# Reordering the way from the last MLP half to the mixture-of-slots layer in a two-layer transformer kernel

## The chip, the cores and the metric

One core of one Trainium2 chip runs the whole program in one launch, all data in float32 (a few tiles are rounded for TensorE). The metric is device time in microseconds (us), the median of several executions.

## The reference

Four sequences (batches) of 1024 tokens with 256 channels pass two layers; each layer's two blocks have the form x = x + gate * f(h), where h is the layer norm of x, scaled and shifted by six rows that a condition vector gives.

- Layer 0: causal softmax attention with 16 heads of 64, then a low-rank MLP with gelu.
- Layer 1, first block: layer norm, linear-time attention (relu features, prefix sums), a residual, layer norm, and an MLP y = gelu(y @ w1 + b1) @ w2 + b2 with 1024 hidden channels.
- Layer 1, second block (the "experts"): tokens are taken in groups of 16. For each group and each of 64 slots the token with the largest logit is chosen, processed and given back:

```
logits = einsum('...btd,des->...btes', grouped, controller) + tie
perm   = (logits == max(logits over the 16 tokens))
sel    = einsum('...btd,...btes->...besd', grouped, perm)
inner  = relu(einsum('...besd,...desf->...besf', sel, f1) + bias)
inter  = einsum('...besf,esfd->...besd', inner, f2)
out    = einsum('...besd,...btes->...btd', inter, perm)
```

The change lies between the MLP and the product with f1.

## The kernel before, in words

The program is written out for four batches, one after the other. `batch(b, carry)` builds one. Every instruction is recorded by `do` of one of five lanes (`pe`, `act`, `dve`, `pool`, `sp`, one an engine), in the order in which the builder calls them, and that is the order on the engine. A step's extra arguments are the steps it waits for; a lane counts its needed steps in one semaphore. There is no planner: the order in which the lines stand sets everything.

A batch has 8 tiles of 128 tokens; a half has 4. For the experts the tiles are grouped as LOW (0 to 3), MIDDLE (4, 5) and HIGH (6, 7). PSUM has 8 banks. `Banks.take` hands them out in turn and gives the step that last read the bank; whoever writes into it waits for that reader. In the traces a bank is named "bank" or "scores", the normalised rows `xn` lie in "hx", as does `h`, `hT3` is "hT", the weights w1 and w2 are "w", the hidden tile is "hid", f1 and f2 are "f", and the logits lie in "inter".

The stretch in question, per batch, in the order of the lines:

- `mlp_wide(1, ...)` (products recorded at L446, gelu at L1011): 8 blocks of hidden channels for tiles 4 to 7. One matmul of the program appears as two records, so a block is 4 records of 512 columns.
- L1512: ScalarE runs an Exp of one column into `spare_column`. Nobody reads it; in front of it the compiler puts the load of the table for Exp, which the next batch's softmax needs. Gelu uses another table; Identity, Copy and Relu need no load in either.
- L1513 `choices(LOW, slot_turn(LOW, ...))`: `turn` transposes the four normalised tiles on TensorE (L420, 4 tiles x 2 channel halves c = 0, 1, one bank for each c), ScalarE copies each bank out with scale and bias (L427). Then `choices` multiplies by the controller (L446, 4 records of 512 columns), and VectorE adds the tie row (L1398), takes the maximum (L1402) and compares (L1403), which gives `permT`. `choice_blocks` (L1413) makes masked copies for the end of the block.
- `mlp_tile(t)` (L1575): 8 matmuls, 16 records of 256 columns, over the hidden channels m = 0 to 7; it is a generator that yields after half of them and at the end. `residual` (L980, L981) then multiplies by the gate row and adds to x on VectorE.
- `spread_choices` (L1526, L1530): turns permT back, one transpose a tile, and VectorE writes `perm`.
- `chosen_rows(tiles, c, ...)` (L1549): 32-row matmuls of `h` by `perm` into four banks, which ScalarE (L1563) or VectorE (L1565) copy into `sel`. For LOW it is called for c = 0 and c = 1 apart, with four ScalarE copies of 128x512 each; for MIDDLE and HIGH with both c at once, eight copies of 128x256, four an engine.
- Norm statistics (L283 to L286 on VectorE), the power -0.5 on GpSimd (L287), the normalisation (L294), `slot_rows_of` (L1381 on VectorE, L1383 on GpSimd), for MIDDLE after tiles 4 and 5, for HIGH after 6 and 7.
- The first expert product (L1629) waits for every copy into `sel`; the second is at L1657. SP loads the next batch's x behind the HIGH logits (`turned_read`).

The order before: wide products, table load, LOW turn and logits, tile 4, LOW spread, tile 5, norm of MIDDLE, tile 6, MIDDLE turn, half of tile 7, MIDDLE logits, rest of tile 7, statistics of HIGH, MIDDLE spread, LOW rows c = 0, LOW rows c = 1, HIGH turn, HIGH logits, MIDDLE rows, HIGH spread, HIGH rows, first expert product.

Of the kernel before, what the change touches and what calls it, by code (L numbers as in the profile page):

```python
# [10 lines left out]
ACT = mybir.ActivationFunctionType  # L11
ALU = mybir.AluOpType
# [6 lines left out]
C = D // P  # L19
# [3 lines left out]
TH = T // NH  # L23
# [23 lines left out]
GT = P // NE  # L47
# [60 lines left out]
def build(nc, I, out):  # L108
# [34 lines left out]
    minus_half = sb("minus_half", [P, T])  # L143
# [3 lines left out]
    h, xn = hx[:, 0:T, :], hx[:, T:2 * T, :]  # L147
# [257 lines left out]
    def batch(b, carry):  # L405
# [4 lines left out]
        banks = Banks(all_banks)  # L410
        banks.readers, banks.at = list(carry["readers"]), carry["at"]

        def turn(src, half, ready, dst, scale=None, bias=None, after=None, tiles=None):


            copies, tiles = [], list(tiles or tiles_of(half))
            for c in range(C):
                i, ps, reader = banks.take()
                for n, (t, r) in enumerate(zip(tiles, ready)):
                    done = pe.do(lambda e, n=n, t=t, c=c, ps=ps: nc.tensor.transpose(  # L420
                        ps[:, n * P:(n + 1) * P], src[:, t, c * P:(c + 1) * P], ident[:, :]), r, reader)
                ps = ps[:, 0:len(tiles) * P]
                o = dst[:, c, tiles[0] * P:(tiles[-1] + 1) * P]
                if scale is None:
                    copy = act.do(lambda e, o=o, ps=ps: nc.scalar.copy(o, ps), done, after)
                else:
                    copy = act.do(lambda e, o=o, ps=ps, c=c: nc.scalar.activation(  # L427
                        o, ps, ACT.Identity, bias=bias[:, c:c + 1], scale=scale[:, c:c + 1]), done, after)
                banks.read_by(i, copy)
                copies.append(copy)  # L430
            return copies
# [941 lines left out]
                last = e.dma_start(f2[k * EF:(k + 1) * EF, :, :], f2_dram[k]).then_inc(loaded["f2"], 16)  # L1373
            return last

        def slot_turn(tiles, normed):
            return turn(xn, None, normed, hT3, scale=mod_cols[:, 1, 4, :, b], bias=mod_cols[:, 1, 3, :, b], tiles=tiles)

        def slot_rows_of(tiles, normed):

# [27 lines left out]
        def choice_blocks(tiles):  # L1408

            cols = columns(tiles)  # L1410
            for k in range(2):
                view = [a[:, cols].rearrange("p (q two t) -> p q two t", two=2, t=NE)[:, :, k, :] for a in (blockT, permT)]
                step = dve.do(lambda e, view=view, k=k: nc.vector.tensor_scalar(  # L1413
                    view[0], view[1], half_mask[:, k:k + 1], None, op0=ALU.mult), perm_done[tiles[0]])
            block_done.update({t: step for t in tiles})
# [93 lines left out]
        slots_normed = [normalise(x, 0, mlp_output(0, wide0), EPS)]  # L1509
        slots_h = slot_rows_of(LOW, slots_normed[0])  # L1510
        wide1 = mlp_wide(1, mlp_turn(1, mlp_norms[1]))
        act.do(lambda e: nc.scalar.activation(spare_column[:, :], minus_half[:, 0:1], ACT.Exp))  # L1512
        choices(LOW, slot_turn(LOW, slots_normed[0]))  # L1513
        choice_blocks(LOW)


        sel_done, sel_product = [], []

        def spread_choices(tiles):

# [17 lines left out]
        def chosen_rows(tiles, c, ready, engines):  # L1538

            half, first = tiles[0] // TH, tiles[0] % TH  # L1540
            taken = [banks.take() for r in range(QR)]

            def emit(e):
                for n, t in enumerate(tiles):
                    for k, cc in enumerate(c):
                        for r, (i, ps, reader) in enumerate(taken):
                            rows_ = slice(r * VPAD, (r + 1) * VPAD)
                            at_ = (k * len(tiles) + n) * P
                            last = nc.tensor.matmul(ps[:, at_:at_ + P], h[rows_, t, cc * P:(cc + 1) * P],  # L1549
                                                    perm[half][rows_, first + n, :, :].rearrange("p g s -> p (g s)"),  # L1550
                                                    start=True, stop=True)
                return last

            done = pe.do(emit, *ready, *[reader for i, ps, reader in taken])
            sel_product.append(done)
            yield
            for r, (i, ps, reader) in enumerate(taken):
                at_ = half * TH * GT + r * 2 * TH + 2 * first
                for k, cc in enumerate(c):
                    o = sel[:, cc, :, at_:at_ + 2 * len(tiles)]  # L1560
                    src = ps[:, k * len(tiles) * P:(k + 1) * len(tiles) * P].rearrange("p (k s) -> p s k", s=ES)
                    if engines[r] == "act":
                        copy = act.do(lambda e, o=o, src=src: nc.scalar.copy(o, src), done)  # L1563
                    else:
                        copy = dve.do(lambda e, o=o, src=src: nc.vector.tensor_copy(o, src), done)  # L1565
                banks.read_by(i, copy)
                sel_done.append(copy)

        def mlp_tile(t):

# [9 lines left out]
            banks.read_by(i, read)  # L1580
            yield wrote

        *_, wrote4 = mlp_tile(TH)
        low_spread = spread_choices(LOW)
        *_, wrote5 = mlp_tile(TH + 1)
        middle_normed = norm_apply(x, norm_stats(x, 1, [wrote4, wrote5], EPS, tiles=MIDDLE))
# [5 lines left out]
        choices(MIDDLE, middle_turned)  # L1592
        wrote7 = next(last_tile)
        inv = norm_stats(x, 1, [wrote6, wrote7], EPS, tiles=HIGH)
        middle_spread = spread_choices(MIDDLE)
        choice_blocks(MIDDLE)
        high_normed = norm_apply(x, inv)
        [*chosen_rows(LOW, (0,), [low_spread, *slots_h], ("act", "act", "act", "act"))]
        second_low = chosen_rows(LOW, (1,), [], ("act", "act", "act", "act"))
        next(second_low)  # L1600
        high_turned = slot_turn(HIGH, high_normed)
        high_h = slot_rows_of(HIGH, high_normed)
        [*second_low]
        turned_read = choices(HIGH, high_turned)
# [16 lines left out]
        for blk in range(4):  # L1621
            i, ps, reader = banks.take()

            def first_product(e, blk=blk, ps=ps):
                for q in range(8):
                    for c in range(C):
                        for k in range(2):
                            s = k * EP + blk * 8 + q
                            last = nc.tensor.matmul(ps[k * EF:(k + 1) * EF, q * G:(q + 1) * G], f1[:, c, s, :], sel[:, c, s, :],  # L1629
                                                    start=c == 0, stop=c == C - 1)  # L1630
                return last

            done = pe.do(first_product, reader, *(sel_done + [(loaded["f1"], 32 * (b + 1))] if blk == 0 else []))
            dst = before_relu[:, blk * 8:blk * 8 + 8, :]
            biased = dve.do(lambda e, ps=ps, dst=dst, blk=blk: nc.vector.tensor_tensor(
                dst, ps.rearrange("p (q g) -> p q g", q=8),
                fbias[:, blk * 8:blk * 8 + 8].unsqueeze(2).to_broadcast([P, 8, G]), op=ALU.add), done)
            banks.read_by(i, biased)

            relu = act.do(lambda e, dst=dst, blk=blk: nc.scalar.activation(  # L1640
                inner[:, blk * 8:blk * 8 + 8, :], dst, ACT.Relu), biased)
            inner_done.append(relu)
# [135 lines left out]
```

## Time and profile before

| | us |
|---|---|
| median of 3 runs | 1891.25 (1889.34 to 1897.14) |
| profiled execution | 1892.87, its span 1891.6 |
| TensorE (PE) busy in the span | 1770.2 |
| VectorE (DVE) busy | 1259.8 |
| ScalarE (ACT) busy | 897.1 |
| GpSimd (POOL) busy | 698.3 |
| mean granted TensorE clock | 0.988 of full speed |

The terms of a sum come from the profiled execution, so they are taken off its own time. In a row of the timeline the columns are: start and duration in us, engine, line, operation, output<-inputs, shapes and count; brackets give the idle time before it and what ended it. Rows of successive instructions of one kind are merged into one.

### The profile page before, as it was taken

How to read it: one execution, taken by the hardware profiler on the slowest of the kernel's cores; microseconds unless marked ns; L12 is line 12 of the kernel's file. 1: busy time of each engine (PE TensorE's matmuls, PEld its weight loads, DVE VectorE, ACT ScalarE, POOL GpSimd, SP SyncE). 2: the span in 40 equal slices, each digit the busy share in tenths (PEclk: the TensorE clock that was granted, in tenths of full speed). 3: DMA queues.
4: the chain of work that ended last, by engine and by line, in shares of the span. 5: the costliest groups of instructions: out<-in, count | busy, mean ns of one | idle time of the engine just before them, and what ended most of it. 6: DMA issues, size and time to landing. Idle time of an engine off the chain costs nothing.

```text
span 1891.6 us, 41279 instructions
## 1 busy us (share of the span) xinstructions
PE 1770.2 (94%) x16417; PEld 1256.2 (66%) x16417; DVE 1259.8 (67%) x2767; ACT 897.1 (47%) x1971; POOL 698.3 (37%) x1090
## 2 busy tenths in 40 slices
PE   7999998998989999999899999999989999999998
PEld 4766785666666667565856666756685666765667
DVE  4688857634688885762578888476367888757545
ACT  4476724223466672423256766242245676533223
POOL 2355543040055564213115555323112555521410
PEclk9899999999999999999999999999999999999999
DMA  8566650050256664023136666303114666520500
GB/s 227 121 153 158 142 159 16 2 89 26 80 143 145 146 139 152 1 37 54 35 95 147 146 142 141 126 1 69 21 36 124 147 147 145 135 98 1 90 1 24
DMA packets 128561, 182.65 MB, mean 97 GB/s; under 512 B 33297, under 2 KB 89329, under 8 KB 127345
## 3 DMA queue, kind: packets, MB, share of 16 engines
q1 hardware_dynamic: 114928, 173.72, 38.0%
q10 hardware_dynamic: 13440, 6.30, 1.2%
q8 instruction: 130, 2.13, 0.5%
q14 instruction: 63, 0.51, 0.1%
HBM read 62.44 MB, written 4.24 MB: 35 GB/s over the span
## 4 chain that ended last, share of the span: by engine, by line
PE 61%; SPq 15%; DVE 12%; ACT 5%; DMA 4%; issue 2%; POOL 0%; DVEq 0%; POOLq 0%
SPq L940 15%; PE scores L446 12%; PE bank L446 7%; PE bank L654 6%; PE scores L634 5%; PE bank L691 4%; DVE prob L768 4%; DMA placed<-prob 3%; PE scores L1657 2%; PE scores L1575 2%; PE scores L1045 2%; ACT prob L868 2%; PE scores L1102 2%; PE scores L1221 1%; PE bank L707 1%
## 5 line engine op out<-in xcount | busy, mean ns | idle before, releaser
L868 ACT ACTIVATE prob<-prob,neg_max 128x768 f32<-128x768 f32 (+5 forms) x384 | 273.6, 714 | 95.3 <-DVE neg_max L760 95.3
L654 PEld LDWEIGHTS bank<-placed,v_t 128*64 128x64 f32 x4608 | 252.3, 137 | 92.9 <-issue 92.9
L654 PE MATMUL bank<-placed,v_t 128*64 128x128 f32 x4608 | 274.4, 275 | 32.6 <-DMA placed<-prob 24.6
L634 PE MATMUL scores<-k_t,q_t 64*128 64x128 f32 (+10 forms) x2176 | 287.9, 410 | 0.0
L287 POOL TENSOR_TENSOR rstd<-rstd,minus_half 128x2 f32<-128x2 f32 x96 | 69.5, 725 | 574.8 <-DVE rstd L286 574.4
L768 DVE STREAM_TRANSPOSE prob<-prob 128x1536 f32<-128x1536 f32 x128 | 225.3, 1772 | 29.6 <-ACT prob L868 28.8
L830 POOL COPY placed<-prob 32x768 f32<-32x768 f32 x256 | 210.8, 823 | 19.6
L634 PEld LDWEIGHTS scores<-k_t,q_t 64*128 64x128 f32 x2176 | 165.0, 187 | 71.8 <-issue 61.2
L760 DVE CUSTOM_DVE_ANT_1 prob<-scores,hx 128x128 f32<-128x128 f32 (+4 forms) x320 | 165.3, 576 | 54.3 <-PE scores L634 34.0
L817 POOL COPY rec_wide<-rec 128x128 f32<-128x128 f32 x256 | 65.4, 291 | 329.5 <-DVE rec L772 232.8
L868 ACT ACTIVATE hx<-hx,neg_max 128x896 f32<-128x896 f32 (+1 forms) x128 | 119.5, 934 | 77.4 <-DVE neg_max L760 76.7
L760 DVE CUSTOM_DVE_ANT_1 hx<-scores,hx 128x896 f32<-128x896 f32 (+1 forms) x128 | 114.8, 953 | 51.8 <-PE scores L634 46.3
L768 DVE STREAM_TRANSPOSE hx<-hx 128x1536 f32<-128x1536 f32 x64 | 110.5, 1760 | 9.9 <-ACT hx L868 9.8
L830 POOL COPY placed<-hx 32x768 f32<-32x768 f32 x128 | 105.4, 823 | 9.7
L691 PE MATMUL bank<-hT,w_ring 128*128 128x512 f32 x224 | 103.6, 605 | 0.0
L1011 ACT ACTIVATE hid<-scores,b 128x512 f32<-128x512 f32 x96 | 62.9, 694 | 64.2 <-PE scores L446 64.2
L980 DVE TENSOR_TENSOR tmp<-bank,mod_rows 128x256 f32<-128x256 f32 x26 | 11.0, 425 | 122.1 <-PE bank L1031 64.0
L446 PE MATMUL scores<-mT,w 128*128 128x512 f32 x192 | 85.8, 596 | 3.5 <-ACT mT L427 3.5
L839 POOL TENSOR_TENSOR yT<-yT,tmp 128x256 f32<-128x256 f32 (+1 forms) x64 | 46.1, 730 | 113.5 <-ACT yT L881 113.5
L881 ACT COPY yT<-bank 128x256 f32<-128x256 f32 (+2 forms) x128 | 44.0, 369 | 84.5 <-PE bank L654 84.4
L760 DVE CUSTOM_DVE_ANT_0 prob<-scores,hx 128x1024 f32<-128x1024 f32 x64 | 75.8, 1222 | 6.6 <-PE scores L634 6.6
L1230 DVE TENSOR_TENSOR am<-scores,tril 128x512 f32<-128x512 f32 x112 | 69.9, 683 | 11.8 <-PE scores L1221 8.7
(246 smaller groups left out, 3330.3 us busy)
## 6 DMA issues: line engine op xcount, KB each, us to landing
placed<-prob SPq DMA_DIRECT2D x768, 96.0 KB, 2.2
placed<-hx SPq DMA_DIRECT2D x384, 96.0 KB, 2.1
f<-in_L_ffn_f SPq DMA_DIRECT2D x16, 2048.0 KB, 13.3
x<-in_L_attn_x SPq DMA_DIRECT2D x8, 512.0 KB, 4.3
mod_rows<-mod_scratch SPq DMA_DIRECT2D x32, 128.0 KB, 5.7
out<-x SPq DMA_DIRECT2D x16, 256.0 KB, 2.2
w_ring<-in_L_attn_w_q ACTq DMA_DIRECT2D x24, 128.0 KB, 2.9
w_ring<-in_L_attn_w_kv_up ACTq DMA_DIRECT2D x48, 64.0 KB, 2.2
```

The source lines that it names most:

```text
L287: step = pool.do(lambda e, ts=ts: nc.gpsimd.tensor_tensor(rstd[:, ts], rstd[:, ts], minus_half[:, ts], op=ALU.pow), var, filled)
L446: step = pe.do(lambda e, n=n, w=w, m=m: nc.tensor.matmul(ps, w, m, start=n == 0, stop=n == len(pieces) - 1), copy, *after)
L634: last = nc.tensor.matmul(score_tiles[head][:, at_ // 512, at_ % 512:at_ % 512 + count], q_t[buf][rows_, tile * P:(tile + 1) * P], k_of[bu ...
L654: last = nc.tensor.matmul(out_bank[rows_, at_:at_ + P], v_t[pair % 2][:, j, rows_], placed[m % 2][:, :, head, first_block(m, i) + j, :], s ...
L691: last = nc.tensor.matmul(ps, ring[:, c * P:(c + 1) * P], hT[:, c, cols], start=c == 0, stop=c == C - 1)
L760: nc.vector.tensor_tensor_reduce(prob[m % 3][:, :, head, blocks, :].rearrange("p g n i -> p g (n i)"), src.rearrange("p (g m) -> p g m", g ...
L768: nc.vector.transpose(p_, p_).then_inc(flow["shuffled"], 1)
L817: last = nc.gpsimd.tensor_copy(rec_wide[:, out_slot(m, tile), :].rearrange("p (a n) -> p a n", a=HEADS), rec[:, at_:at_ + HEADS].unsqueeze ...
L830: nc.gpsimd.tensor_copy(placed[m % 2][rows_, g, :, :, :], prob[m % 3][rows_, g, :, :, :]).then_inc(flow["kept"], 1)
L868: nc.scalar.activation(p_, p_, ACT.Exp, scale=-1.0, bias=neg_max[:, k:k + 1], accum_out=row_sum[:, k:k + 1]).then_inc(flow["exp_done"], 1)
L940: e.dma_start(placed[m % 2][target * GROUP:(target + 1) * GROUP, source, :, :, :], prob[m % 3][source * GROUP:(source + 1) * GROUP, target ...
L1230: masked.append(dve.do(lambda e, r=r, ps=ps: nc.vector.tensor_tensor(am[t % 2][:, r * 4:r * 4 + 4, :], ps.rearrange("p (h n) -> p h n", h= ...
```

## The change

- `turn` and `slot_turn` have a new argument `shared`; with it the bank of c = 1 is copied by VectorE (tensor_scalar with a scale and a bias column) and not by ScalarE. Only the HIGH turn sets it.
- The LOW turn stays where it was. Behind it now stands the first half of tile 4, then LOW logits and blocks, then the table load, then the rest of tile 4.
- The LOW rows for c = 0 stand ahead of the MIDDLE spread.
- `sel_done` is kept by c, and the copies into `sel` run over c outside and banks inside; a bank's reader is its last copy. The first expert product waits for all of them, as before.

```diff
-        def turn(src, half, ready, dst, scale=None, bias=None, after=None, tiles=None):
+        def turn(src, half, ready, dst, scale=None, bias=None, after=None, tiles=None, shared=False):
...
                 if scale is None:
                     copy = act.do(lambda e, o=o, ps=ps: nc.scalar.copy(o, ps), done, after)
+                elif shared and c:
+                    copy = dve.do(lambda e, o=o, ps=ps, c=c: nc.vector.tensor_scalar(
+                        o, ps, scale[:, c:c + 1], bias[:, c:c + 1], op0=ALU.mult, op1=ALU.add), done, after)
                 else:
...
-        act.do(lambda e: nc.scalar.activation(spare_column[:, :], minus_half[:, 0:1], ACT.Exp))
-        choices(LOW, slot_turn(LOW, slots_normed[0]))
-        choice_blocks(LOW)
-        sel_done, sel_product = [], []
+        low_turned = slot_turn(LOW, slots_normed[0])
+        sel_done, sel_product = {c: [] for c in range(C)}, []
...
-            for r, (i, ps, reader) in enumerate(taken):
-                at_ = half * TH * GT + r * 2 * TH + 2 * first
-                for k, cc in enumerate(c):
+            for k, cc in enumerate(c):
+                for r, (i, ps, reader) in enumerate(taken):
+                    at_ = half * TH * GT + r * 2 * TH + 2 * first
...
-                banks.read_by(i, copy)
-                sel_done.append(copy)
+                    banks.read_by(i, copy)
+                    sel_done[cc].append(copy)
...
-        *_, wrote4 = mlp_tile(TH)
+        first_tile = mlp_tile(TH)
+        next(first_tile)
+        choices(LOW, low_turned)
+        choice_blocks(LOW)
+        act.do(lambda e: nc.scalar.activation(spare_column[:, :], minus_half[:, 0:1], ACT.Exp))
+        wrote4 = next(first_tile)
         low_spread = spread_choices(LOW)
...
         inv = norm_stats(x, 1, [wrote6, wrote7], EPS, tiles=HIGH)
+        [*chosen_rows(LOW, (0,), [low_spread, *slots_h], ("act", "act", "act", "act"))]
         middle_spread = spread_choices(MIDDLE)
         choice_blocks(MIDDLE)
         high_normed = norm_apply(x, inv)
-        [*chosen_rows(LOW, (0,), [low_spread, *slots_h], ("act", "act", "act", "act"))]
         second_low = chosen_rows(LOW, (1,), [], ("act", "act", "act", "act"))
         next(second_low)
-        high_turned = slot_turn(HIGH, high_normed)
+        high_turned = slot_turn(HIGH, high_normed, shared=True)
...
-            done = pe.do(first_product, reader, *(sel_done + [(loaded["f1"], 32 * (b + 1))] if blk == 0 else []))
+            done = pe.do(first_product, reader, *(sel_done[0] + sel_done[1] + [(loaded["f1"], 32 * (b + 1))] if blk == 0 else []))
```

## Rows read from the trace of the kernel before

**Rows 1.** The page, busy us (share of the span) and instructions of each engine.
```profile
PE 1770.2 (94%) x16417; PEld 1256.2 (66%) x16417; DVE 1259.8 (67%) x2767; ACT 897.1 (47%) x1971; POOL 698.3 (37%) x1090
```

**Rows 2.** Timeline of ScalarE, batch 0, behind the last gelu.
```profile
428.36 1.28 ACT L1512 ACT_TABLE_LOAD   x1
429.65 0.20 ACT L1512 ACTIVATE spare_column<-minus_half 128x1 f32<-128x1 f32 x1
429.76 1.43 ACT L427 ACTIVATE hT<-scores,mod_cols 128x512 f32<-128x512 f32 x2
445.93 1.02 ACT L427 ACTIVATE hT<-scores,mod_cols 128x256 f32<-128x256 f32 x2 [14.74 <-PE scores L420]
```

**Rows 3.** Timeline of TensorE, from the low transposes to the low spread, batches 0 and 2.
```profile
427.45 1.04 PE L420 MATMUL scores<-ident,hx 128*128 128x128 f32 x8
...
437.64 0.46 PE L1526 MATMUL scores<-ident,permT 64*128 64x64 f32 x4
...
1356.28 1.04 PE L420 MATMUL scores<-ident,hx 128*128 128x128 f32 x8
1359.41 1.98 PE L446 MATMUL bank<-hT,ctrl 128*128 128x512 f32 x4 [2.09 <-ACT hT L427]
1361.23 3.62 PE L1575 MATMUL bank<-w,hid 128*128 128x256 f32 x16
1364.78 0.46 PE L1526 MATMUL scores<-ident,permT 64*128 64x64 f32 x4
```

**Rows 4.** Busy us by stretch: total, PE, PEld, DVE, ACT, POOL, then granted clock, DMA.
```profile
431.00:434.00 3.00, 3.00 (x5) 1.11 (x4) 0.00 (x0) 0.19 (x1) 0.00 (x0) 0.50 0.00 0
1359.40:1364.80 5.40, 5.39 (x21) 3.74 (x21) 2.69 (x5) 0.62 (x1) 0.00 (x0) 1.00 0.00 0
1387.00:1390.00 3.00, 1.47 (x28) 1.17 (x24) 2.16 (x8) 1.20 (x4) 0.00 (x0) 0.50 0.53 179
1390.00:1393.00 3.00, 2.82 (x53) 2.85 (x55) 0.32 (x2) 0.00 (x0) 0.00 (x0) 0.50 0.02 5
```

**Rows 5.** Timeline, VectorE behind the low logits (batch 2), and middle permT and spread (batch 0).
```profile
1361.43 0.69 DVE L1398 TENSOR_TENSOR inter<-bank,tie 128x512 f32<-128x512 f32 x1 [13.84 <-PE bank L446]
...
1362.88 0.69 DVE L1403 TENSOR_TENSOR permT<-inter,logit_max 128x512 f32<-128x512 f32 x1
...
449.66 0.42 DVE L1403 TENSOR_TENSOR permT<-inter,logit_max 128x256 f32<-128x256 f32 x1
450.36 0.33 PE L1526 MATMUL bank<-ident,permT 64*128 64x64 f32 x2
```

**Rows 6.** Timeline of TensorE, batch 0, from second low rows to first expert product.
```profile
453.11 0.38 PE L1549 MATMUL scores<-perm,hx 32*128 32x128 f32 x2 [1.31 <-DVE perm L1530]
...
454.22 0.66 PE L420 MATMUL scores<-ident,hx 128*128 128x128 f32 x4
455.31 1.16 PE L446 MATMUL scores<-hT,ctrl 128*128 128x256 f32 x4 [0.44 <-ACT hT L427]
457.31 0.39 PE L1549 MATMUL scores<-perm,hx 32*128 32x128 f32 x3 [0.84 <-ACT sel L1563]
...
458.41 0.33 PE L1526 MATMUL bank<-ident,permT 64*128 64x64 f32 x2
459.33 1.17 PE L1549 MATMUL scores<-perm,hx 32*128 32x128 f32 x32 [0.58 <-DVE perm L1530]
462.23 5.20 PE L1629 MATMUL scores<-sel,f 128*64 128x64 f32 x128 [1.73 <-DVE sel L1565]
```

**Rows 7.** The same stretch: timeline of ScalarE and VectorE, and L1565's durations.
```profile
454.69 1.02 ACT L427 ACTIVATE hT<-scores,mod_cols 128x256 f32<-128x256 f32 x2 [0.78 <-PE scores L420]
...
458.54 1.20 ACT L1563 COPY sel<-scores 128x256 f32<-128x256 f32 x4 [0.89 <-PE bank L1549]
...
453.46 0.74 DVE L294 TENSOR_SCALAR hx<-x,mv,rstd 128x256 f32<-128x256 f32 x2
...
L1565 DVE COPY sel<-scores x24: 414/415/425, 459.1 to 1850.4; 128x256 f32<-128x256 f32 x24
```

More of the change, by code:

```diff
@@ L1374, in load_f2, with slot_turn @@
             return last
-        def slot_turn(tiles, normed):
-            return turn(xn, None, normed, hT3, scale=mod_cols[:, 1, 4, :, b], bias=mod_cols[:, 1, 3, :, b], tiles=tiles)
+        def slot_turn(tiles, normed, shared=False):
+            return turn(xn, None, normed, hT3, scale=mod_cols[:, 1, 4, :, b], bias=mod_cols[:, 1, 3, :, b], tiles=tiles,
+                        shared=shared)
         def slot_rows_of(tiles, normed):
```

## The prediction

> **What bounds the kernel now.** I read the page first: busy time by engine and the chain that ended last. TensorE is busy 94% of the span [rows 1] and heads the chain too, so time can only be won where it stands still or runs at the low clock. The change touches one place, which the program passes four times (once a batch): from the last wide products of the second MLP half to the first expert product. So I then read the timeline of that place, engine by engine, in batch 0 (about 427 to 462 us) and in batch 2, and last the granted clock.
>
> Three things are to be seen. First, ScalarE: behind the last gelu stand a table load of 1.28 us and its column of 0.20, and only then the two copies of the turned rows [rows 2]. TensorE idles 2.09 us for the first of them, in all four batches alike [rows 3]. Second, TensorE's clock: in batch 0, behind that idle time, 431 to 434 us ran at 0.50 of full speed, the lower of the two levels (1.2 of 2.4 GHz); batch 1 shows the same. In batch 2 the same idle time was followed by full clock [rows 3, 4], as in batch 3. From the start of the eight transposes to that of the spread transposes took 10.19 us in batches 0 and 1 and 8.50 in 2 and 3 [rows 3]: one fall of the clock costs 1.69 us. Third, the tail from 453 to 462 us is a chain of short handovers PE, ACT, PE, DVE, with TensorE idle 1.31, 0.44, 0.84, 0.58 and 1.73 us [rows 6, 7]. It too is followed by a low clock, in each of the four batches (batch 2's rows are shown) [rows 4].
>
> **Part 1: table load behind the logits, half an MLP tile ahead of them.** I work in batch 2, which has no fall here. The transposes end at 1357.32. Products start about 0.16 before their forerunner's modelled end (logits end 1361.39, the tile starts 1361.23), so the first half of tile 4 starts at 1357.16. It is 8 of 16 products; the tile takes 3.55 us up to the next group [rows 3], so the half takes 1.78: to 1358.94. Its gelu inputs, m 0 to 3, are long done. Meanwhile ScalarE starts the copies right behind the last gelu. In batch 0 that is 428.36, and both take 1.43, to 429.79, where the logits would be reached at 428.49 - 0.16 + 1.78 = 430.11 [rows 2, 3]. The half tile therefore hides both copies with 0.3 us over, and the 2.09 us of idle time goes. The logits take 1.98: end 1360.92. VectorE follows 0.04 later, and add, maximum and comparison take 2.14 (1361.43 to 1362.88 + 0.69) [rows 5]: permT at 1363.10. The second half tile ends at about 1360.76 + 1.78 = 1362.54, so now **permT is late**, where before the full tile covered it. From permT's end to the spread transposes it was 0.28 in the middle group (449.66 + 0.42 to 450.36) [rows 5]; I take the same: 1363.38, against 1364.78. Gain 1.40 us, with a new idle stretch of 0.8 us.
>
> The table load itself keeps its 1.48 us but stands behind the low copies, where ScalarE was idle 14.74 us [rows 2]; were that cover gone, the most it could cost is its 1.48 us a batch. VectorE's residual of tile 4 comes earlier too, but still behind choice_blocks; it ends long before tile 5 does. No DMA and no queue is passed here; SP's load of next_x follows the logits of the last tiles as before.
>
> In batches 0 and 1 the same 6.22 us from the transposes' end (less 0.16) count: 428.49 + 6.06 = 434.55 against 437.64, gain 3.09, provided that the clock no longer falls. I take that it does not, since the idle stretch that preceded the fall is gone. Sum of part 1: 2 x 3.09 + 2 x 1.40 = **8.98 us**. Below, the bound is 4 x 1.40 = 5.6 if the clock falls as often as before.
>
> By the Trainium skill (TensorE: Matmul & The Clock Gate, Part 4: PE-mode transpose) transposes do not count as activity the way products do. That speaks against the change in one spot: the new 0.8 us of idle time is followed by four spread transposes. The same page (What's actually happening) calls the count of slow products variable from run to run of one kernel. No row here shows either by itself; by the first the clock could fall behind the spread, and the sum would be the rival "given back" below.
>
> **Part 2: low rows ahead of the middle spread.** The first chosen_rows(LOW) no longer stands behind the middle permT, and the second one waited for the bank that the middle spread had used: its reader, perm, stood on VectorE behind the statistics, 1.31 us of idle TensorE at 453.11 [rows 6]. Now that bank is one that ScalarE copies first, and the wait ends some 0.9 us earlier. It is worth nearly nothing: next in line are the HIGH transposes, and their rows are ready only at 453.46 + 0.74 = 454.20, which the transposes met at 454.22 anyway [rows 6, 7]. That chain (statistics, POOL, norm) is unchanged. I take 0, bounds 0 to 0.1.
>
> **Part 3: last turned rows copied by two engines.** Both ScalarE copies take 454.69 to 455.71. VectorE's copy of the second half starts when the transposes end, 454.22 + 0.66, and costs between 0.37 (a tensor_scalar from SBUF: 0.74 for two) and 0.42 (a copy of 128x256 from PSUM, 0.415) [rows 6, 7]. I take 0.42, the row that also reads PSUM: ready at 455.34. The first half's products last until about 455.6 anyway, so the logits gain 0.15 to 0.2. More is won on ScalarE: its copies of the second low rows start 0.5 earlier, and the middle rows on TensorE waited for these (0.84 idle before 457.31). They, and the spread behind them (458.41), come 0.5 earlier [rows 6, 7]. VectorE's slot rows are held up by 1.2 us by the copy ahead of them; POOL still ends their additions near 457.3, before the HIGH rows want them (459.33).
>
> Against that stands the reordered loop of sel copies: the bank of the middle rows' r0 is now released by the third ScalarE copy, not the second, a step of 0.3 (four take 1.20) [rows 7]. Copies start at 458.04 instead of 458.54, the third ends near 458.95; perm alone would be ready at 458.7. So the HIGH rows start at about 459.05 against 459.33, and what follows keeps its distance: gain 0.28. Bounds: 0.5 (whole gain kept) and -0.3 (ScalarE no earlier, release later). I take 0.3 a batch, **1.2 us** in all.
>
> **Sum.** 8.98 + 0 + 1.2 = 10.2 us. The profiled execution took 1892.87 us (span 1891.6): 1882.7 after. It stood 1.6 above the median of the runs, 1891.25, so the median after is **1881.1 us**. What this kernel's measurement can tell from no change is 0.5%, 9.5 us: down to 1881.8, so the forecast lies just beyond it.
>
> **The rivals.**
> *Given back in the clock.* The fall moves rather than goes: behind the new 0.8 us stretch at the spread, or one fall more in the tail. For it: the tail has low clock behind it in every batch, and in batch 2 twice as long, from before the HIGH rows [rows 4]; work comes at other moments than before. Against it: behind 1.31 us of idle time at 453.11 no fall was seen. With two to four falls of 1.69: 1884.5 to 1887.9.
> *The tail gives nothing or costs.* The longer held bank and VectorE's fuller queue eat part 3: 4 x -0.3 in place of +1.2, 1883.5.
> *More is won.* Batch 2's longer low stretch (1387 to 1393 us, so 3 us more of low clock at half speed, some 1.5, plus slower handovers) does not occur and the tail keeps 0.5: 1881.1 - 1.5 - 0.8 - 1.0 = 1878.
> *Slower.* The mechanism is the clock again, in the tail: it falls before the HIGH rows and stays low for twice as long, as in batch 2, in every batch, and once more behind the spread. It needs over six new falls (10.2 / 1.69) to lose the gain, and eleven or so to be slower by more than 0.5%; with eight, 1894.6. Nothing in the four batches shows that many.
>
> **Chances.** Forecast case (gain 8.5 to 12) 0.55, of which 0.40 lies beyond 0.5%; given back 0.20; tail gives nothing 0.12; more won 0.10; slower 0.03. So faster 0.50, same 0.46, slower 0.04. Range 1876.5 to 1887: its low end is "more won" less the scatter of a median (the runs shown spread over 8 us, two of them within 2), its high end nearly all of "given back".
>
> **What would show it.** Behind the eight transposes MLP products without idle time, and the table load behind both low copies. The distance from the transposes to the low spread 7.1 us in all batches, with 0.8 us of idle time before the spread and full clock. TensorE's wait before the second low rows near 0.5, before the middle rows near 0.3 to 0.4; 0.3 us less from the HIGH transposes to the first expert product. Wrong would be: a granted clock of 0.5 between transposes and spread; idle time before the logits; or a tail as long as before.

## The result, and the profile after

| | median us | runs |
|---|---|---|
| before | 1892.11 (1889.34 to 1897.14) | 5 |
| changed | 1877.29 (1875.05 to 1879.73) | 5 |

The ratio is 0.9915, interval 0.9901 to 0.9928: faster by 14.8 us between the medians, where the forecast was a gain of 10.2. The profiled execution took 1879.73 us, the longest of its five, and 13.1 less than that of before. TensorE has as many records as it had and the same share of the span [rows 1], but is busy 4.7 us less: the same products took less time, which is a first sign of the clock. The rest of the 13.1 is idle time. The page of the changed kernel, busy us by engine:

```profile
PE 1765.5 (94%) x16417; PEld 1253.3 (67%) x16417; DVE 1261.6 (67%) x2771; ACT 895.0 (48%) x1967; POOL 698.3 (37%) x1090
```

ScalarE in batch 0, changed kernel (start, duration, engine, line, operation; answers to [rows 2]). Both low copies start right behind the last gelu, the table load behind them:

```profile
427.91 0.69 ACT L1014 ACTIVATE hid<-scores,b 128x512 f32<-128x512 f32 x1 [1.03 <-PE scores L449]
428.50 1.44 ACT L430 ACTIVATE hT<-scores,mod_cols 128x512 f32<-128x512 f32 x2
429.95 1.28 ACT L1589 ACT_TABLE_LOAD   x1
431.25 0.20 ACT L1589 ACTIVATE spare_column<-minus_half 128x1 f32<-128x1 f32 x1
```

TensorE from the low transposes to the low spread (answers to [rows 3]): no idle time before the logits, 0.51 us before the spread, 6.71 us in all.

```profile
427.71 1.04 PE L420 MATMUL scores<-ident,hx 128*128 128x128 f32 x8
428.58 1.89 PE L1577 MATMUL bank<-w,hid 128*128 128x256 f32 x8
430.31 1.88 PE L449 MATMUL bank<-hT,ctrl 128*128 128x512 f32 x4
432.03 1.89 PE L1577 MATMUL bank<-w,hid 128*128 128x256 f32 x8
434.42 0.46 PE L1528 MATMUL scores<-ident,permT 64*128 64x64 f32 x4 [0.51 <-DVE permT L1407]
```

VectorE behind the low logits (answers to [rows 5]): permT ends at 434.37, and the spread starts 0.05 us later.

```profile
432.23 0.69 DVE L1402 TENSOR_TENSOR inter<-bank,tie 128x512 f32<-128x512 f32 x1 [13.20 <-PE bank L449]
...
433.68 0.69 DVE L1407 TENSOR_TENSOR permT<-inter,logit_max 128x512 f32<-128x512 f32 x1
```

The tail of batch 0 on TensorE (answers to [rows 6]). The idle times are 0.53, 0.42, 0.44, 0.41, 0.86 and 1.73 us:

```profile
449.12 0.38 PE L1551 MATMUL scores<-perm,hx 32*128 32x128 f32 x2 [0.53 <-DVE stats L283]
...
450.71 0.87 PE L420 MATMUL scores<-ident,hx 128*128 128x128 f32 x4 [0.42 <-DVE hx L294]
452.02 1.13 PE L449 MATMUL scores<-hT,ctrl 128*128 128x256 f32 x4 [0.44 <-ACT hT L430]
453.56 0.39 PE L1551 MATMUL scores<-perm,hx 32*128 32x128 f32 x3 [0.41 <-ACT sel L1565]
...
454.67 0.33 PE L1528 MATMUL bank<-ident,permT 64*128 64x64 f32 x2
455.86 1.17 PE L1551 MATMUL scores<-perm,hx 32*128 32x128 f32 x32 [0.86 <-DVE sel L1567]
458.76 5.44 PE L1636 MATMUL scores<-sel,f 128*64 128x64 f32 x128 [1.73 <-DVE sel L1567]
```

VectorE and ScalarE beside it (answers to [rows 7]): the shared copy at L427 takes 0.54 us, and perm ends at 455.46, while the HIGH rows start at 455.86. They take over the bank that the third of the four ScalarE copies reads last; that copy ends at 455.72. The profile names VectorE's first copy into sel, which ends at 455.79, but reads no bank that the HIGH rows take.

```profile
451.62 0.54 DVE L427 TENSOR_SCALAR hT<-scores,mod_cols 128x256 f32<-128x256 f32 x1 [0.64 <-PE scores L420]
...
455.04 0.42 DVE L1532 TENSOR_TENSOR perm<-bank,par_mask 128x256 f32<-128x256 f32 x1 [0.51 <-PE bank L1528]
```
```profile
454.79 1.20 ACT L1565 COPY sel<-scores 128x256 f32<-128x256 f32 x4 [0.89 <-PE bank L1551]
```

Last the granted clock (answers to [rows 4]; columns as there, the granted clock third from the end). It is full from the low transposes to the spread. Behind the tails of batches 0 and 3 it is 0.50, behind those of batches 1 and 2 it is 1.00:

```profile
427.70:434.40 6.70, 6.22 (x29) 4.49 (x27) 2.07 (x3) 3.51 (x5) 0.00 (x0) 1.00 0.00 0
459.00:462.00 3.00, 3.00 (x61) 3.00 (x61) 0.00 (x0) 0.00 (x0) 0.00 (x0) 0.50 0.00 1
917.90:920.90 3.00, 3.00 (x103) 3.00 (x105) 0.82 (x2) 0.16 (x1) 0.00 (x0) 1.00 0.03 5
1379.40:1382.40 3.00, 2.86 (x92) 2.72 (x92) 0.79 (x2) 0.19 (x1) 0.00 (x0) 1.00 0.03 5
1838.00:1841.00 3.00, 3.00 (x58) 3.00 (x60) 0.04 (x1) 0.00 (x0) 0.00 (x0) 0.50 0.02 5
```

To account for the time I cut each batch of each trace at four starts on TensorE: T, the eight low transposes; S, the low spread; F, the first expert product; G, the second expert product. From F to G takes 7.62 us at full clock (batch 1 of the changed kernel below); where it takes over 8.5 I call the tail low.

```profile
917.89 3.95 PE L1636 MATMUL scores<-sel,f 128*64 128x64 f32 x128 [1.73 <-DVE sel L1567]
...
925.51 1.67 PE L1664 MATMUL scores<-inner,f 64*128 64x64 f32 x26
```

| trace | T to S, batches 0 to 3 | S to F | F to G | T to G, sum |
|---|---|---|---|---|
| before | 10.19 10.19 8.50 8.50 | 24.6 24.6 25.4 24.6 | 8.86 9.05 9.07 9.06 | 172.6 |
| changed | 6.71 6.72 6.71 6.72 | 24.3 24.3 24.3 24.3 | 9.10 7.62 7.99 9.02 | 157.9 |

T to G gained 14.7 us; the stretches outside it lost 1.5. That is about one fall of the clock, and the changed kernel has one near 1162 us which the trace of before lacks. Of the 14.7, T to S gave 10.5, S to F 1.8 and F to G 2.3, where not one instruction differs.

### The profile page after: what moved, and what is told of

Same layout as the page of the kernel before. It is cut to its first block, busy times and chain, and to the rows that moved or that the text cites. A ratio compares the mean times of both kernels' runs of the same rounds, so it can differ in the third digit from the quotient of the medians.

```text
span 1878.5 us, 41287 instructions
## 1 busy us (share of the span) xinstructions
PE 1765.5 (94%) x16417; PEld 1253.3 (67%) x16417; DVE 1261.6 (67%) x2771; ACT 895.0 (48%) x1967; POOL 698.3 (37%) x1090
## 4 chain that ended last, share of the span: by engine, by line
PE 62%; SPq 14%; DVE 13%; ACT 5%; DMA 4%; issue 2%; POOL 1%; DVEq 0%; POOLq 0%
SPq L943 14%; PE scores L449 12%; PE bank L449 7%; PE bank L657 6%; PE scores L637 5%; PE bank L694 4%; DVE prob L771 4%; DMA placed<-prob 3%; PE scores L1664 2%; PE scores L1577 2%; PE scores L1048 2%; ACT prob L871 2%; PE scores L1105 2%; PE scores L420 1%; PE scores L1224 1%
```

## The experiments

All changes are edits of the changed kernel or of the kernel before. Times are medians of 4 to 12 runs where nothing else is said; each is compared with the kernel before on the same chip. The traces show one execution each.

**Part 1 alone.** The middle spread again ahead of the low rows, the HIGH turn by ScalarE alone, banks outside and halves inside in the copies into sel.

```diff
-            for k, cc in enumerate(c):
-                for r, (i, ps, reader) in enumerate(taken):
+            for r, (i, ps, reader) in enumerate(taken):
+                for k, cc in enumerate(c):
...
-        [*chosen_rows(LOW, (0,), [low_spread, *slots_h], ("act", "act", "act", "act"))]
         middle_spread = spread_choices(MIDDLE)
         choice_blocks(MIDDLE)
         high_normed = norm_apply(x, inv)
+        [*chosen_rows(LOW, (0,), [low_spread, *slots_h], ("act", "act", "act", "act"))]
...
-        high_turned = slot_turn(HIGH, high_normed, shared=True)
+        high_turned = slot_turn(HIGH, high_normed)
```

> Part 1 alone (table load behind the low logits, tile 4 in two halves around them); low rows behind the middle spread, HIGH turn copied by ScalarE alone and the order of the copies into sel are as before the change. Theory A (the changed kernel's surplus over my 10 us is the clock in the tail, and the clock in the tail is a matter of the moment, not of parts 2 and 3): 6.7 us from transposes to low spread in each batch, from the middle transposes to the first expert product 16.98 as before; about 1.0 us slower than the changed kernel by instructions, 1878 to 1881 us, and low stretches in the tail in some batches only. Rival B (parts 2 and 3 keep the clock up by shortening the tail's idle time): low clock behind the tail in all four batches, as before the change, 1882 to 1885 us, mean clock 0.989 to 0.990.

Measured: 1877.35 us (1872.77 to 1880.28), before 1890.95, ratio 0.9932 (0.9911 to 0.9952). By the trace 6.71 us from T to S, 31.30 from T to F in every batch against 31.05 of the changed kernel: parts 2 and 3 are worth 0.25 us a batch, 1.0 in all, which the median does not resolve. The tail looks as before the change, and its clock was low behind batches 0 to 2 and full behind batch 3 (windows behind the tails of batches 1 and 3):

```profile
917.50:920.50 3.00, 3.00 (x64) 3.00 (x60) 0.00 (x0) 0.00 (x0) 0.00 (x0) 0.50 0.02 5
1838.00:1841.00 3.00, 3.00 (x104) 3.00 (x106) 0.79 (x2) 0.19 (x1) 0.00 (x0) 1.00 0.02 5
```

So B is out: one tail of the old form kept its clock, and the time is 4.7 us under B's range, just under A's. Three low tails of four here and four of eight in the changed kernel (two traces) are too few to say that parts 2 and 3 do nothing for the clock.

**Tile 4 whole behind the low logits.** The table load stays behind them.

```diff
-        first_tile = mlp_tile(TH)
-        next(first_tile)
         choices(LOW, low_turned)
         choice_blocks(LOW)
         act.do(lambda e: nc.scalar.activation(spare_column[:, :], minus_half[:, 0:1], ACT.Exp))
-        wrote4 = next(first_tile)
+        *_, wrote4 = mlp_tile(TH)
```

> The changed kernel with tile 4 whole behind the low logits; the table load stays behind them. Theory A: TensorE idles about 0.7 us (last gelu to first copied half) instead of 2.09 before; transposes to low spread 7.1 us in all batches at full clock, so 0.4 us a batch slower than the changed kernel: 1878 to 1880 us. Rival (the clock needs the half tile there): at least one batch falls to 0.5 behind the 0.7 us gap, 8.8 us there, and the time is 1881 us or more.

Measured: 1874.63 us (1872.36 to 1877.59), ratio 0.9922 (0.9902 to 0.9941). Batch 0 on TensorE:

```profile
428.01 1.04 PE L420 MATMUL scores<-ident,hx 128*128 128x128 f32 x8
429.62 1.98 PE L449 MATMUL bank<-hT,ctrl 128*128 128x512 f32 x4 [0.57 <-ACT hT L430]
431.44 3.62 PE L1577 MATMUL bank<-w,hid 128*128 128x256 f32 x16
434.99 0.46 PE L1528 MATMUL scores<-ident,permT 64*128 64x64 f32 x4
```

Idle 0.57 us instead of 2.09, no fall in four batches, T to S 6.98. The table load's move alone therefore gives 1.52 us a batch plus the clock; the half tile adds 0.27, as it trades 0.57 us of idle time for 0.51 ahead of the spread. The median is 3.4 us under what I expected and even under that of the changed kernel (1877.29, and 1875.96 when it ran again): the 1.1 us that the half tile gives by the trace (4 x 0.27) drown in the scatter, and the medians show no worth of it.

**The first gap of the kernel before filled.** Four products that nobody reads, between low transposes and logits.

```diff
+        def idle_products(count):
+
+            i, ps, reader = banks.take()
+
+            def emit(e):
+                for n in range(count):
+                    last = nc.tensor.matmul(ps[:, 0:D], w1[:, 0, 0:P], w2[:, 0, :], start=True, stop=True)
+                return last
+
+            banks.read_by(i, pe.do(emit, reader))
+
...
-        choices(LOW, slot_turn(LOW, slots_normed[0]))
+        low_turned = slot_turn(LOW, slots_normed[0])
+        idle_products(4)
+        choices(LOW, low_turned)
```

> The kernel before with four more products (128x256, into a bank that nobody reads) between the low transposes and the low logits, so that TensorE's idle time there falls from 2.09 to about 0.35 us; nothing else moves. It tells the clock's share of part 1 by itself. Theory A: transposes to low spread 8.50 us in all four batches and never 10.19; against the kernel before a gain of 1.69 us for each fall it had there (two of four in the profile), 1888 to 1890 us. Rival: the clock is not governed by that idle time; still falls in some batches, 1891 to 1893 us.

Measured: 1884.15 us (1880.88 to 1887.36, 12 runs) against 1890.95 (17 runs), ratio 0.9965 (0.9952 to 0.9979). Batch 0:

```profile
427.58 1.89 PE L1519 MATMUL bank<-w 128*128 128x256 f32 x8
429.84 1.98 PE L446 MATMUL bank<-hT,ctrl 128*128 128x512 f32 x4 [0.36 <-ACT hT L427]
...
435.21 0.46 PE L1539 MATMUL scores<-ident,permT 64*128 64x64 f32 x4
```

T to S is 8.50 in all batches, as expected. But 6.8 us is twice what I expected: work that computes nothing, in a kernel whose every step kept its length at full clock, gained 0.35%. F to G read 7.85, 7.62, 7.62 and 8.79: three of four tails had kept their clock. Here my view that the tail's clock is the same on both sides failed. With the further traces of both kernels below, three of each, T to G takes 171.6 us before and 164.6 with the gap filled: 3.4 us less at the low logits and 3.7 less in the tail, together near the 6.8.

**The changed kernel's tail filled.**

```diff
+        idle_products(4)
         inner_done = []
```

> The changed kernel with four more products (128x256, bank read by nobody) behind the HIGH rows, in the 1.73 us that TensorE waits for the last copies into sel. They end at about the time these do, so by instructions they cost 0 to 0.2 us a batch. Theory A (the low clock under the first expert products comes from TensorE's idle time in the tail, 1.7 us a fall): no low stretch behind any tail, first to second expert product 7.4 to 7.6 us in all batches, and the time falls by 1.5 us for each fall that the changed kernel has (two in its profile): 1873 to 1876 us. Rival: the fall is decided by the whole tail or by something else, and stays: 1877 to 1879 us.

Measured: 1873.42 us (1869.95 to 1875.99), ratio 0.9911 (0.989 to 0.9932). The filler and what follows it, batch 0, and the clock under the expert products of batches 0 and 3:

```profile
454.84 1.99 PE L1633 MATMUL scores<-w 128*128 128x256 f32 x8
456.76 2.08 PE L1648 MATMUL scores<-sel,f 128*64 128x64 f32 x64
```
```profile
457.00:464.00 7.00, 7.00 (x242) 6.98 (x240) 2.07 (x3) 1.89 (x3) 0.00 (x0) 1.00 0.02 5
1834.00:1841.00 7.00, 7.00 (x248) 7.00 (x245) 2.07 (x3) 1.89 (x3) 0.00 (x0) 1.00 0.02 5
```

No low clock behind a tail, F to G 7.82 and three times 7.62; the filler costs 0.12 us a batch. A holds.

**The changed kernel again.**

> The changed kernel once more, beside the next three. The four profiles so far leave 8.2 us (2.04 a batch) of the 14.8 to the order of the work and the rest to a lower clock seen less often. Theory A (the order gives 8.2 us in every execution, the clock the rest and it varies): transposes to first expert product 31.05 us in all four batches again, first to second expert product 7.6 to 9.2 us by chance, median 1875 to 1878 us. Rival (the clock behind the tail is fixed by the order): again low behind batches 0 and 3 and not behind 1 and 2.

Measured: 1875.96 us (1872.01 to 1876.62) against 1890.04, ratio 0.9923 (0.9907 to 0.9939). T to F 31.05 in all batches; F to G 9.16, 7.62, 8.98 and 7.62: low behind batches 0 and 2, not 0 and 3. The order of the work doesn't fix where it falls.

**The kernel before filled at both places** (the two edits above, on the kernel before).

> The kernel before with both idle times filled by four products that nobody reads: between low transposes and low logits, and behind the HIGH rows. The same tail filler in the changed kernel gave 1873.4. Theory A (14.8 us are 8.2 of order and some 6.6 of clock): with the clock full in both, what is left between them is the order: 1881 to 1883 us, transposes to first expert product 33.2 us in every batch and 7.6 to 7.9 behind. Rival (the gain is the order alone, larger than I count, and the clock averages out): 1887 to 1889 us.

Measured: 1882.93 us (1880.18 to 1886.93), ratio 0.9961 (0.9946 to 0.9976). T to S 8.50, T to F 33.2, F to G 7.61 in all four batches, T to G 163.3 in sum; the filled changed kernel had 155.3. With the clock full from T to G on both sides the order is worth 8.0 us in the traces (9.5 between the medians, which come from two chips).

**The low spread half a tile later.** The remaining 0.51 us of idle time.

```diff
-        low_spread = spread_choices(LOW)
-        *_, wrote5 = mlp_tile(TH + 1)
+        second_tile = mlp_tile(TH + 1)
+        next(second_tile)
+        low_spread = spread_choices(LOW)
+        wrote5 = next(second_tile)
```

> The changed kernel with the first half of tile 5 ahead of the low spread, so that it covers the 0.51 us for which the spread waits for permT. Theory A (the wait is exposed and nothing behind needs perm early): no idle time there, 0.5 us a batch from transposes to middle transposes, 2.0 us in all: 2 us under the changed kernel beside it. Rival (VectorE becomes late: tile 4's residual and perm stand ahead of tile 5's residual): under 0.2 us a batch.

Measured: 1872.03 us (1869.7 to 1879.06), ratio 0.9912 (0.9892 to 0.9933), 3.9 us under the changed kernel beside it. Batch 0, no idle time around the spread:

```profile
432.68 1.89 PE L1577 MATMUL scores<-w,hid 128*128 128x256 f32 x8
434.50 0.46 PE L1528 MATMUL scores<-ident,permT 64*128 64x64 f32 x4
434.89 5.45 PE L1577 MATMUL scores<-w,hid 128*128 128x256 f32 x24
```

T to F 30.48 us, 0.57 less a batch, 2.3 in all, which is the order's part. No tail was low in this trace, against two in the changed kernel's beside it; that the rest of the 3.9 is clock is likely but not shown, as a second trace of this kernel (below) has two low tails.

**A combined version:** late spread, the old loops in the copies into sel, three idle products in the tail.

> A version meant to beat both: the changed kernel with the late low spread (0.51 us a batch), the copies into sel in the order of before (banks outside, halves inside; the middle rows' first bank is free one ScalarE copy earlier, 0.27 us a batch by the handovers) and three idle products behind the HIGH rows. Theory A: 30.3 us from transposes to first expert product, full clock behind each tail, 1869 to 1871 us. Rival (the reordered loop is not what holds the HIGH rows): HIGH transposes to first expert product stay 8.05 us, 1871 to 1873 us.

Measured: 1870.72 us (1868.83 to 1871.88), ratio 0.99 (0.9883 to 0.9916). Batch 0, from the HIGH transposes:

```profile
450.59 0.87 PE L420 MATMUL scores<-ident,hx 128*128 128x128 f32 x4 [0.42 <-DVE hx L294]
...
455.46 1.17 PE L1551 MATMUL scores<-perm,hx 32*128 32x128 f32 x32 [0.58 <-DVE perm L1532]
456.57 1.56 PE L1635 MATMUL scores<-w 128*128 128x256 f32 x6
458.37 2.09 PE L1650 MATMUL scores<-sel,f 128*64 128x64 f32 x64 [0.23 <-DVE sel L1567]
```

With the old loops the HIGH rows wait 0.58 us, for perm, instead of 0.86: H to F is 7.78 against 8.05. The new loop order costs 0.27 us a batch. T to F 30.20.

**Two more traces of the kernel before, and a second one of it with its gap filled.**

> The kernel before, unchanged, for a second trace. Filling its first idle time alone was worth 6.8 us, where the first trace shows only 2 x 1.69 = 3.4 us lost there. Theory A1 (the number of falls at the low logits varies; the first trace had fewer than most): three or four batches with 10.2 us from transposes to low spread. Rival A2 (two of four is usual, but with the gap unfilled the tail falls more often too): two such batches and a low stretch behind all four tails, first to second expert product 8.8 us or more in each.

> The kernel before once more, for a third trace; as for the one ahead: A1 expects three or four falls at the low logits, A2 two, with all four tails low. A mixture would leave the share open.

> The kernel before with its first gap filled, once more, for a second trace. A1 expects no fall at the low logits and the tail as in any trace, two to four falls; A2 expects the tail to fall rarely (one of four in the first trace): none to two.

Measured (one run each): 1893.1 and 1890.94 us; two falls at the low logits in each (batches 0 and 3), three and four low tails. The filled one 1887.01, with none at either place; its T to G took 162.8 us, the least of the three traces with the gap filled, and its stretches outside 1722.9 us, the most. So the forecast's two falls of four were typical, six of twelve in three traces, and A1 is out. What the first trace could not tell is that the tail's falls are fewer in other forms of the kernel.

**The combined version without idle products.**

> The combined version without its idle products: late low spread and the copies into sel in their order of before. The idle products cost 0.12 us a batch by the traces. Theory A (with the late spread the tail's clock stayed up in four of four, by chance or not, without filler): 30.1 us from transposes to first expert product; if the clock stays up, 1869 to 1871 us, as the combined version or 0.5 under it. Rival (the filler is what keeps the tail at full clock): low stretches behind one to three tails and 1872 to 1875 us, with a wider scatter than the combined version's 3 us.

Measured: 1871.13 us (1870.3 to 1871.82), ratio 0.9892 (0.9876 to 0.9909). T to F 30.2 to 30.4, F to G 7.61, 7.62, 8.04 and 7.62. As fast as with the filler, and with as little scatter; in these four runs the filler was not needed. By its ratio it is 20 us under the kernel before, and it stands about 5 us under the changed one (1875.96, beside the combined version).

**Does the tail depend on the gap ahead of it?** First the kernel before with its tail alone filled, then the changed kernel with one product pair in its 0.51 us gap.

```diff
+        idle_products(1)
         low_spread = spread_choices(LOW)
```

> The kernel before with idle products behind the HIGH rows alone; its first idle time of 2.09 us stays. Three traces of the kernel before have two falls of four at the low logits and eleven low stretches behind twelve tails. Theory C1 (the two places fall independently): the tail is at full clock, 7.6 us from first to second expert product in all batches, and two batches fall at the low logits; some 1.4 us saved for each of four tails, 0.5 us paid for the filler: 1885 to 1887 us. Rival C2 (a quiet stretch at one place also decides at the other): no falls at the low logits either, 1882 to 1884 us.

> The changed kernel with one more product pair (0.43 us, read by nobody) in the 0.51 us for which the low spread waits. Filling the 2.09 us gap of the kernel before had left its tail at full clock in seven of eight batches, 25 us later. Theory C2 (quiet time there lets the tail fall): tail at full clock in three or four batches, transposes to first expert product 31.05 to 31.2 us, 1873 to 1875 us. Rival C1 (it is a matter of the moment at which the tail comes): falls behind two or so tails as in the changed kernel, 1876 to 1877.5 us.

> The kernel before with its first gap filled, for a third trace. C2: none or one low stretch behind four tails, as in the two traces before (one of eight). C1: two or more.

> The changed kernel with the late low spread, for a second trace; the first had no low stretch behind four tails. C2 (the 0.51 us of idle time is gone, so the tail keeps its clock): none or one. C1: two or more.

Measured: the filled tail 1888.62 us (1886.29 to 1894.54, 12 runs), before 1890.87, ratio 0.9986 (0.9971 to 1.0002), slower than either theory had it, and not told apart from the kernel before; no low clock from F to G, yet three falls at the low logits. In batch 3, the one without, the clock fell inside the tail, ahead of the first expert product: from the HIGH transposes to F it took 9.75 us, in the others 8.14.

```profile
1842.00:1843.00 1.00, 1.00 (x21) 0.78 (x16) 0.18 (x1) 0.00 (x0) 0.00 (x0) 0.50 0.00 0
```

So the filler didn't do away with every fall in the tail.

The filled small gap 1877.17 us (1873.9 to 1884.57), ratio 0.9929 (0.991 to 0.995): four low tails of four, batches 0 and 1 shown. The trace is of its slowest execution, 1884.57 us, so four may be more than is usual for it.

```profile
458.00:461.00 3.00, 3.00 (x68) 3.00 (x67) 0.07 (x1) 0.00 (x0) 0.00 (x0) 0.58 0.02 5
918.00:921.00 3.00, 3.00 (x63) 3.00 (x61) 0.00 (x0) 0.00 (x0) 0.00 (x0) 0.50 0.02 5
```

The gap-filled kernel again (one run): 1881.92 us, two low tails. The late spread again (one run): 1873.28 us, two. C2 is refuted: no quiet time at the low spread, and yet four low tails, and a median in C1's range of 1876 to 1877.5 and above C2's. C1 as I put it, the two places independent of each other, does not explain the count either:

| kernels (traces) | falls at the low logits | low from F to G |
|---|---|---|
| before (3) | 6 of 12 | 11 of 12 |
| before, gap filled (3) | 0 of 12 | 3 of 12 |
| before, tail filled (1) | 3 of 4 | 0 of 4 (one fall just ahead of F) |
| changed, its part 1, tile whole, small gap filled (5) | 0 of 20 | 13 of 20 |
| late spread, with either loop order (3) | 0 of 12 | 2 of 12 |
| both places filled, or changed with filled tail (3) | 0 of 12 | 0 of 12 |

## Why the prediction fell short

The direction and the mechanism of part 1 were right, the size too small. The median itself, 1877.29, lies within 1876.5 to 1887, but with two more runs of the kernel before its median is 0.9 us above the one that the forecast quotes. Against the 1891.25 that the forecast starts from, the ratio 0.9915 is 16 us (1875.2), just beyond the 14.75 of the range's low end.

The step that failed is the tail's part of the sum: it holds 1.2 us for the order and nothing for the clock, though the prediction itself reads a low clock behind all four tails, and it gives no reason why that should stay as it was. The runs showed 2.3 us there. A second term, T to S, was 1.6 us too small.

Over two traces of the changed kernel and three of before, T to G took 157.7 and 171.6 us. That is 13.9 us, and the full-clock lengths divide it: at full clock it is 4 x (33.08 + 7.62) = 162.8 before and 4 x (31.05 + 7.62) = 154.7 changed. The difference, 8.1, is the order's; what the traces have above these lengths is the clock's.

| term | forecast | measured |
|---|---|---|
| order, T to S | 4 x 1.40 = 5.6 | 4 x 1.79 = 7.2 |
| order, tail | 1.2 | 4 x 0.25 = 1.0 |
| clock at the low logits | 3.4 | 3.4 |
| clock in the tail | 0 | 2.3 |
| sum | 10.2 | 13.9 |

- **The gap before the logits goes, both copies are hidden, the table load is hidden:** right, to 0.1 us [rows 2, 3].
- **"From permT's end to the spread transposes it was 0.28 in the middle group; I take the same":** wrong, it was 0.05. In [rows 5] TensorE was not waiting for a signal. The row ahead of that spread on TensorE in the kernel before, tile 7's second half, ran until 450.43 and filled the whole "handover":

```profile
448.54 1.89 PE L1575 MATMUL scores<-w,hid 128*128 128x256 f32 x8
450.36 0.33 PE L1526 MATMUL bank<-ident,permT 64*128 64x64 f32 x2
```

  The half tile (1.73 for 1.78) and the logits (1.88 for 1.98) were each taken 0.05 to 0.1 us too long as well. Together 0.39 us a batch, 1.6 of the miss.
- **The new idle time before the spread:** right, but 0.51 us and not 0.8, for the same reason.
- **Low rows ahead of the middle spread, worth nothing:** right. The wait fell from 1.31 to 0.53 us, and the HIGH transposes start 0.29 us earlier, but they end no more than 0.1 earlier, waiting in their midst for the second normalised row tile.
- **The tail, 0.3 a batch:** 0.25. The middle rows' wait fell from 0.84 to 0.41, and the third-copy release took 0.27 back, as worked out; the combined version shows both. VectorE's shared copy took 0.54 us, outside my bounds of 0.37 and 0.42, at no cost, since the first half's products covered it. The 0.37 was misread as well: 0.74 is the length of two that overlap, and each takes 0.41.
- **Clock at the low logits, two falls of 1.69:** right in size; three traces of before have six falls in twelve batches, all kernels without the gap of 2.09 us none in 56.
- **The term that was not there is the tail's clock.** "What follows keeps its distance" was true of instructions only. Three traces of before lost 5.4 us a run there and two of the changed kernel 3.1. I had filed it under "more is won" and had let only batch 2's longer stretch go, with 0.10.

The Trainium skill's rule that speaks against the change (TensorE: Matmul & The Clock Gate, Part 4: PE-mode transpose) left room for a fall behind the 0.51 us of idle time and the four spread transposes. In the 16 batches with this order and an open gap (four traces) the clock never fell there, which neither bears the rule out nor refutes it. The same page's other remark (What's actually happening), that the count of slow products varies from run to run of one kernel, fits what these traces show: the changed kernel was low behind batches 0 and 3 in one trace, 0 and 2 in the next.

What stays open: why the kernel before falls behind nearly every tail (11 of 12) and the same tail with a filled gap 28 us ahead rarely (3 of 12). The idle time inside the tail has a part in it: with it filled, none of 16 was low from F to G. But the tail's idle times are the same with the gap filled and unfilled, and filling the 0.51 us at the spread didn't help. The moment at which the tail comes may be all there is to the rest; no experiment set that moment by itself. The four batches of a trace aren't independent draws, so the counts are rough.

## What to carry to other kernels

Work put into an idle stretch of TensorE is paid twice where the clock falls behind it: once the wait, once 1.2 to 1.7 us for a stretch at half speed. So count idle stretches, take several traces, and give the clock a term of its own for every such stretch, also for those that the change leaves alone. Before a "handover" is read off two starts, look whether the waiting engine was busy until then. When a wait is covered by moved work, ask at once what waits next: here half a tile more ahead of the low spread won another 2.3 us, and the old loop order another 1.1.

## What the runs showed of the hardware

- Twelve us of spread between runs of one unchanged kernel (1883.84 to 1895.76 in 15) go with the granted clock: 0.990 in the shortest of them, 0.986 and 0.987 in the two longest, and a straight line in the clock takes up some four fifths of the variance. By the traces one low stretch costs 1.7 us at the low logits and 1.2 to 1.5 from F to G.
- Eight product records a batch that nobody reads, in one idle stretch, made the kernel before 6.8 us faster (1884.15 against 1890.95).
- A VectorE tensor_scalar with two column operands, 128x256 from PSUM, took 0.54 us, where the plain copy of the same shape took 0.415 [rows 7].
- The table load takes 1.28 us in its new place too, and the next ScalarE instruction starts 0.02 behind it.
